# Second attention of an eight-sample transformer block: the product of probabilities and keys in groups of 3, 3, 3 and 4 row tiles

## The reference

```python
q_hk = (hidden_q @ Wq.T).reshape(b, s, H, K)
q_big = jnp.einsum('bshk,hkq->bshq', q_hk, w_kc_q)
kv_rope = kv_c * cos[None] + _rotate_half(kv_c) * sin[None]
q_r = jnp.einsum('bshq,hqr->bhsr', q_big, W_qr)
k_r = jnp.einsum('bld,hdr->bhlr', kv_rope, W_kr)
scores = jnp.einsum('bhsr,bhlr->bhsl', q_r, k_r)
attn = jax.nn.softmax(scores, axis=-1)
ctx_c = jnp.einsum('bhsl,bld->bhsd', attn, kv_rope)
ctx_lat = jnp.einsum('bhsd,hkd->bshk', ctx_c, w_kc_kv)
out = ctx_lat.reshape(b, s, H * K) @ Wo.T
```

## Time and profile before

| what | us |
|---|---|
| median of 3 runs (lowest to highest) | 866.58 (866.45 to 871.25) |
| profiled execution | 868.13 |
| its span, first to last instruction | 866.3 |
| TensorE busy in the span | 718.5 (83%) |
| VectorE, ScalarE, GpSimd busy | 510.5, 416.7, 248.4 |
| second attention, first score tile to first fold matmul | 427.78 to 664.15 |

### The profile page before, as it was taken

The page is one execution under the profiler, slowest core; times in us unless marked ns, Lnnn a source line. Parts: engine busy times, 40 slices in busy tenths (PEclk is TensorE's granted clock), DMA queues, the critical chain, the costliest instruction groups (busy, mean ns, idle before and its releaser), DMA issues.

```text
span 866.3 us, 13037 instructions
## 1 busy us (share of the span) xinstructions
PE 718.5 (83%) x4421; PEld 566.6 (65%) x4427; DVE 510.5 (59%) x1037; ACT 416.7 (48%) x777; POOL 248.4 (29%) x279
## 2 busy tenths in 40 slices
PE   0799999636999999985989989989996688799974
PEld 0597777425777777875868778778774265566541
DVE  4876675675666666156664564663663333677683
ACT  3523665345555555212575574664674312455552
POOL 2000931222112220342183282372451000122232
PEclk9987999667999999965999999999999789999997
DMA  8546732896675555983001212222425781111000
GB/s 260 200 173 202 256 106 85 294 343 234 206 228 176 167 163 164 332 220 105 2 25 45 63 44 63 63 55 51 130 66 109 246 358 67 50 50 37 13 25 15
DMA packets 82932, 118.90 MB, mean 137 GB/s; under 512 B 41761, under 2 KB 59933, under 8 KB 79297
## 3 DMA queue, kind: packets, MB, share of 16 engines
q1 hardware_dynamic: 79745, 109.71, 39.5%
q0 software_dynamic: 3136, 8.53, 3.7%
HBM read 97.15 MB, written 27.62 MB: 144 GB/s over the span
## 4 chain that ended last, share of the span: by engine, by line
PE 44%; issue 23%; DVE 11%; POOL 9%; ACT 6%; DMA 5%; SPq 1%; ACTq 1%; POOLq 0%; DVEq 0%
PE PS L149 9%; PE PS L151 8%; PE PS L150 8%; POOL wraw L818 6%; PE PS L1225 3%; PE PS L1286 3%; PE PS L1572 2%; DMA fq_raw<-foldq_in 2%; ACT w_hi L871 2%; PE PS L1329 2%; DMA raw<-wkv_in 1%; PE PS L1538 1%; ACT cx_hi L1113 1%; PE PS L1269 1%; PE PS L1318 1%
## 5 line engine op out<-in xcount | busy, mean ns | idle before, releaser
L818 POOL TENSOR_TENSOR wraw<-wraw,rinv 128x361 f32<-128x361 f32 (+1 forms) x104 | 80.8, 790 | 138.9 <-DVE rinv L1786 138.9
L1629 DVE TENSOR_TENSOR w_lo<-w,w_hi 128x1408 fp32r<-128x1408 f32 x40 | 65.0, 1625 | 38.5 <-ACT w_hi L871 38.5
L967 ACT ACTIVATE wraw<-PS,nmx 128x361 f32<-128x361 f32 (+1 forms) x104 | 58.7, 565 | 38.2 <-DVE nmx L1793 30.4
L1793 DVE TENSOR_REDUCE nmx<-PS 128x1 f32<-128x361 f32 (+1 forms) x104 | 55.0, 530 | 33.6 <-PE PS L151 33.6
L846 POOL TENSOR_TENSOR wraw<-gs,us 128x352 f32<-128x352 f32 (+1 forms) x28 | 26.6, 951 | 153.6 <-ACT gs L1141 125.9
L871 ACT CAST w_hi<-w 128x1408 fp32r x40 | 54.7, 1370 | 18.9 <-issue 9.8
L770 POOL DMA_INDIRECT xb<-xn_scratch,rows x20 | 32.7, 1634 | 105.4 <-PE PS L1197 102.3
L149 PE MATMUL PS<-w_hi,xt_hi 128*128 128x352 f32 x160 | 56.7, 355 | 6.2 <-DVE xt_lo L1623 6.0
L1796 DVE TENSOR_TENSOR pt_lo<-PS,pt_hi 128x384 fp32r<-128x384 f32 x96 | 52.3, 547 | 12.0 <-ACT pt_hi L973 11.1
L149 PE MATMUL PS<-pf_hi,cx_hi 128*128 128x512 f32 (+1 forms) x112 | 48.3, 431 | 11.5 <-DVE pf_lo L1964 4.5
L1385 PE MATMUL PS<-ident,wraw 128*128 128x128 f32 x312 | 52.1, 277 | 6.4 <-POOL wraw L818 3.7
(11 more groups left out here) (277 smaller groups left out, 1996.0 us busy)
## 6 DMA issues: line engine op xcount, KB each, us to landing
w<-w_in SPq DMA_DIRECT2D x20, 768.0 KB, 5.6
w<-w_in SPq DMA_DIRECT2D x8, 1408.0 KB, 11.3
fq_raw<-foldq_in SPq DMA_DIRECT2D x6, 1088.0 KB, 7.6
ctx_scratch<-ctxo SPq DMA_DIRECT2D x24, 256.0 KB, 2.1
cx_raw<-tile_scratch SPq DMA_DIRECT2D x6, 1024.0 KB, 4.9
ys_scratch<-yb SPq DMA_DIRECT2D x20, 256.0 KB, 5.6
wraw<-wup_in SPq DMA_DIRECT2D x12, 256.0 KB, 4.3
w1q<-w_scratch SPq DMA_DIRECT2D x1, 2816.0 KB, 11.2
```

The costliest lines, as they stand in the source:

```text
L818: pool.tensor_tensor(P1[slot][0:rows, 0:NK], P1[slot][0:rows, 0:NK], rinv[0:rows, jj, t:t + 1].broadcast_to((rows, NK)), ALU.mult).then_in ...
L967: act.activation(P1[t % 8][r, 0:NK], PS[r, t % 4, 0:NK], ACT.Exp, bias=nmx[r, jj, t:t + 1], accum_out=rsum[r, jj, t:t + 1]).then_inc(C["ex ...
L1629: dve.tensor_tensor(WL[which][:, :], w12_of(dve_wlo.e, which), WH[which][:, :].bitcast(F32), ALU.subtract) \
L1793: dve.tensor_reduce(nmx[r, jj, t:t + 1], PS[r, t % 4, 0:NK], AX.X, ALU.max, negate=True).then_inc(C["max"], 1)
```

## The change

The groups hold 3, 3, 3 and 4 tiles: 384, 384, 384 and 448 columns. `group_of` and `group_cols` give the group of a tile and its width. The third pair of buffers is dropped, and the two others are 448 columns wide and alternate by group number (g % 2); since NG stays 4, each batch begins with buffer 0. ScalarE waits for buffer g % 2 until the product of group g - 2 is done. Thirds of the first three groups stand two, three and four steps behind the turn of tiles 2, 5 and 8; those of the last group 4 steps behind tile 12, all in one step, as before. The stores have 384 or 448 columns.

```diff
-NG = -(-RT // 4)
+NG = RT // 3
...
-        PTH = [sc_(f"pt_hi{i}", [128, LK, 512], F32R) for i in range(2)]
-        PTL = [sc_(f"pt_lo{i}", [128, LK, 512], F32R) for i in range(2)]
-        PTH.append(sc_("pt_hi_end", [128, LK, ROWS % 512], F32R))
-        PTL.append(sc_("pt_lo_end", [128, LK, ROWS % 512], F32R))
+        PTH = [sc_(f"pt_hi{i}", [128, LK, ROWS - 384 * (NG - 1)], F32R) for i in range(2)]
+        PTL = [sc_(f"pt_lo{i}", [128, LK, ROWS - 384 * (NG - 1)], F32R) for i in range(2)]
...
-                    if t % 4 == 3:
-                        due += [(at + PVLAG + c, 0, ("PV", b, t // 4 * LK + c)) for c in range(LK)]
-                    elif t == RT - 1:
-                        due += [(at + PVLAG + 2, 0, ("PV", b, t // 4 * LK + c)) for c in range(LK)]
+                    if t == RT - 1:
+                        due += [(at + PVLAG + 2, 0, ("PV", b, (NG - 1) * LK + c)) for c in range(LK)]
+                    elif t % 3 == 2 and t // 3 < NG - 1:
+                        due += [(at + PVLAG + c, 0, ("PV", b, t // 3 * LK + c)) for c in range(LK)]
...
+        def group_of(t):
+
+            return min(t // 3, NG - 1)
+
+        def group_cols(g):
+
+            return ROWS - 384 * g if g == NG - 1 else 384
...
-                cols = min(512, ROWS - g * 512)
+                cols = group_cols(g)
...
-                    if t % 4 == 0:
-                        wait(act, C["pv"], pt_free(m, t // 4))
-                    act.copy(pt_place(PTH, t, jj), turned(t)).then_inc(C["pth"], 1)
+                    if t == 3 * group_of(t):
+                        wait(act, C["pv"], NG * m + group_of(t) - 1)
+                    act.copy(pt_place(PTH, t), turned(t)).then_inc(C["pth"], 1)
...
-                        wait(pe, C["ptl"], RT * m + min(4 * g + 4, RT))
+                        wait(pe, C["ptl"], RT * m + (3 * g + 3 if g < NG - 1 else RT))
                         wait(pe, C["ctxo"], NG * m + g)
                         wait(pe, C["knl"], m + 1)
```

More of the change, by code:

```diff
@@ L649, in store_ctx @@
             def store_ctx(n, g):
-                cols = min(512, ROWS - g * 512)
+                cols = group_cols(g)
                 wait(sp, C["ctxo"], NG * n + g + 1)
                 dst = ctx_scratch[n] if isinstance(n, int) else ctx_scratch[bass.ds(n, 1)].rearrange("o p r -> (o p) r")
-                sp.dma_start(dst[:, g * 512:g * 512 + cols], ctxo[g % 2][:, 0:cols]).then_inc(C[f"st{g % 2}"], 16)
+                sp.dma_start(dst[:, g * 384:g * 384 + cols], ctxo[g % 2][:, 0:cols]).then_inc(C[f"st{g % 2}"], 16)
             def store_batch(n, j, more=True):
@@ L940, in turned, with pt_place @@
             return PS[:, 4 + t % 3, 0:LK * 128].rearrange("p (c r) -> p c r", c=LK)[:, :, 0:tile_rows(t)]
[L942 to L951, removed]
+        def pt_place(buf, t):
+            at = (t - 3 * group_of(t)) * 128
+            return buf[group_of(t) % 2][:, :, at:at + tile_rows(t)]
         def act_keys(act, n, j):
@@ L977, in act_steps @@
                         continue
-                    cols = min(512, ROWS - t * 512)
+                    cols = group_cols(t)
                     wait(act, C["pv"], NG * m + t + 1)
@@ L1395, in pe_steps @@
                     last = mm3(pe, PS[:, 7, 0:cols], KNH[jj][:, c, :], KNL[jj][:, c, :],
-                               PTH[pt_buffer(g, jj)][:, c, 0:cols], PTL[pt_buffer(g, jj)][:, c, 0:cols], c == 0, c == LK - 1)
+                               PTH[g % 2][:, c, 0:cols], PTL[g % 2][:, c, 0:cols], c == 0, c == LK - 1)
                     if c == LK - 1:
@@ L1795, in dve_steps @@
                     wait(dve, C["pth"], RT * m + t + 1)
-                    dve.tensor_tensor(pt_place(PTL, t, jj), turned(t), pt_place(PTH, t, jj).bitcast(F32), ALU.subtract) \
+                    dve.tensor_tensor(pt_place(PTL, t), turned(t), pt_place(PTH, t).bitcast(F32), ALU.subtract) \
                         .then_inc(C["ptl"], 1)
```

## The result

The kernel with the change takes 853.27 us (median of 6 runs, 850.48 to 855.62), the one before 867.26 in the same comparison (866.45 to 871.25). The ratio is 0.9835, with a 95% interval of 0.9807 to 0.9863: 1.65% faster, where 1.5% was forecast (853.2 against 866.58). In a second comparison, later, it was 851.08 against 867.11, ratio 0.9825 (0.9787 to 0.9864).

What follows compares the result with a forecast made beforehand. TensorE was taken as the first resource, with 5 us of waits per pair. Pairs -3 x 1.2 - 1.4, query steps -3 x 2.1 and tail -2.1 sum to -13.4: 853.2 us against 866.58, forecast range 850 to 857.5, chance 0.6.

Steps and rivals of the forecast that it cites:

- The columns: TensorE's product matmuls: 384 columns take 0.176 us and 448 take 0.202, saving 0.66 us per batch, 5.3 in eight.
- The query steps: Preparation of the next pair's queries, three times: fewer thirds among 64-row matmuls; -2.1 us each, bounds -0.9 and -3.4.
- step 30: Within a pair's query work, numbered 26 to 37: one more product third stands here, +0.5 us.
- The score steps: Score tiles of a pair, numbered 0 to 25: -1.2 us per pair, bounds -0.3 and -2.0; -1.4 in the last pair.
- step 18: Turn 0 of the second batch, at about 516.0 as before; from here through 21, 5.40 us becomes 4.3, sum -1.0.
- steps 22 to 25: End of a pair's score tiles: one third more, a low-half wait gone, four shorter thirds; sum -0.2 us.
- Step 12: Second batch's first score tile waits for the exponential of the last tile, 2.14 us regardless of TensorE's work; sum 0.
- steps 13 to 18: Around the change of batch: low-half waits of 0.46 and 1.04 us go, bank 7 waits replace them; sum 0.
- The tail: Last score tile to fold, once: 12.7 us becomes about 10.5, sum -2.1, bounds -1.2 and -3.0.
- Only the columns: Rival for the whole stage: waits are conserved and only 5.3 us of work is saved; 861.3 us, chance 0.15.
- The partial gain: Rival: query work and tail gain as reckoned, four score stages nothing because ScalarE sets the pace; 858.2 us, chance 0.16.
- The slower rival: Bank 7 waits at group starts: at 1.1 us each the gain is gone, at 1.5 it is 875.2; chance 0.05.

Runs made afterwards that it cites:

- query_late: The changed kernel with the second batch's third-group thirds put back late among the 64-row query matmuls in the first three pairs; 856.28 us, ratio 0.9891.
- turns_on: The changed kernel with the three banks of turned tiles taken in turn across the change of batch, the keys' bank with them; 848.20 us, ratio 0.9794.
- tail_late: The changed kernel with the last pair's second-batch third-group thirds late, the first ahead of turn 12 and the others behind it; 849.13 us, ratio 0.9806.
- two_thirds: The changed kernel with the thirds of a group of three at offsets 0, 1, 1 instead of 0, 1, 2; 855.56 us, ratio 0.9873.

## Why the prediction was right, point by point

- **The columns.** Right, row by row: 0.176 and 0.203 us against the forecast of 0.176 and 0.202. The 64-column matmuls cost nearly half of a 512-column one, and merging them away was worth what the rows said. The Trainium skill, "TensorE: Matmul & The Clock Gate", section "Back-to-back issue gap", would give 0.1625 and 0.189 by its formula for single matmuls, lower than what this trace has for both widths. The prediction set that formula against a stream of matmuls, for which the page does not mean it: for a stream of weight load and matmul it gives about 0.131 at 512 columns. That too is lower than the 0.230 here.
- **The query steps.** Mechanism right, size too small: -2.66 each instead of -2.1. Up to the first 64-row step it was +0.03, as said (13.64 before, 13.67 after). Behind it the measured value is -2.70. The term that was mis-sized is the third among 64-row steps: "I take 1.1 each, -3.3". It came to 1.74 - 0.58 = 1.16 each, and the wait of 0.36 went with it, 3.84 in all. query_late confirms this for 384 columns, 0.99 each. The upper price of 1.42 was a misreading: the two rows that "start 0.32 apart" (482.81, 483.13) are not the starts of two query steps one after the other, but of two that overlap; undisturbed, a step takes 0.58 on average, not 0.32. The group's new third at step 30 cost 0.64 instead of 0.5, and the end +0.67, as taken. These make -2.53. Of the 0.17 that is left, 0.10 is in the same place: from 482.81 to 489.91 before and from 484.98 to 488.13 after, the stretch shrank by 3.95 and not 3.84, since the last three query steps now stand in a row and take 0.50 each (486.62 to 488.13), not 0.58.
- **The score steps.** Right in sign and mostly in the places, too large: -0.97, -0.99 and, in the last pair, -0.84, for -1.2, -1.2 and -1.4. The parts behind step 18 hit: 5.40 became 4.35 (515.14 to 519.49) where 4.3 was forecast, and steps 22 to 25 gave -0.23 for -0.2. Step 12 came out even, as said: the first score tile of the second batch starts 15.28 after S0 before and 15.30 after. What failed is the walk through steps 13 to 18, which ends in "So turn 0 of the second batch comes at about 516.0, as before": it came 0.31 later, counted from S0 (25.08 for 24.77). I had put bank 7 in the place of the vanished waits. Its waits came (0.33, 0.61, 0.33, for "0.5, and 0.8 at step 15"), but what holds turn 0 is the bank of turned tiles that it shares with turn 12, one step ahead. I had looked for what is late next on the product's path only; the turn itself had a second condition, met 0.24 us earlier in the kernel before and so without a wait in any view. VectorE's timeline of the kernel before has it:

```profile
515.36 0.34 DVE L1796 TENSOR_TENSOR pt_lo_end<-PS,pt_hi_end 128x192 fp32r<-128x192 f32 x1
```

  It ends at 515.70, and turn 0 starts at 515.94. The same subtraction in the changed kernel:

```profile
514.63 0.36 DVE L1795 TENSOR_TENSOR pt_lo<-PS,pt_hi 128x192 fp32r<-128x192 f32 x1 [0.23 <-ACT pt_hi L972]
```

  It ends at 514.99, and turn 0 starts at 515.14. Counted from S0, turn 12 itself stands 0.75 us later than before (22.71 for 21.96), behind three thirds more and the waits of 0.33 and 0.61 for bank 7. turns_on, which gives turn 0 another bank, removes the wait.
- **The first pair** gave -0.06 instead of -1.2, and that is the clock: in 425 to 435 us TensorE was granted 0.69 after and 0.83 before. In the repeated run of the changed kernel, where it was 0.83 too, the first pair took 37.34, 1.1 less than before; in query_late, where it was 1.00 throughout the first pair, it took 36.66. The windows of the changed kernel, then of its repeated run:

```profile
425.00:435.00 10.00, 8.59 (x49) 8.02 (x48) 7.29 (x19) 6.89 (x17) 2.71 (x4) 0.69 0.01 2
```

```profile
425.00:435.00 10.00, 8.75 (x44) 8.09 (x45) 7.78 (x24) 8.11 (x24) 7.27 (x10) 0.83 0.01 2
```

- **The tail.** Right, -2.09 for -2.1, and for the reason given. The last group began at 8.66 us after the last score tile where 8.6 was estimated. What I did not see is that the early place is not the best one (tail_late).
- **Outside the stage** +1.6 and -1.7 us cancel; both are in code that the change does not touch. In the repeated run the first S0 came at 425.43, 2.35 earlier than that of the kernel before, so the +1.6 is scatter.
- **The sum** of -13.4 met -13.0 because the score steps fell short by 2.1 us (of which 1.1 in the first pair) and the query steps ran over by 1.7. That the total was hit within 0.1 us is luck, since the two medians of the changed kernel (853.27, 851.08) lie 2.2 apart; the signs and the places are not.
- **The rivals.** "Only the columns" had the score steps nearly right (PE's busy time fell by 0.7 per pair, the idle time by 0.3) but falls with the query steps. The partial gain (no gain in the four score stages, because ScalarE sets the pace) falls with the 0.8 to 1.0 us that three of the four gained, and its reason falls with turns_on, where another 1.54 came from a bank alone. The slower rival asked for waits of 1.1 at each start of a group on bank 7; the longest was 0.61, and two_thirds, which has none of these waits, gains nothing.
- **A sign that was badly chosen.** The prediction asked for "the second pair's first score tile at 487.9 instead of 491.17" and took "behind 489.5" as the sign that the columns were nearly all. It came at 490.06 and by this sign the forecast was wrong. In the repeated run it came at 485.07. An absolute time carries all the scatter ahead of it. The distance between the S0 of two pairs is free of it in the later ones: 62.84 before, 59.20 after, -3.6 for a forecast of -3.3.

## What to carry to other kernels

When a wait disappears, list every condition of the instructions behind it, also those met just in time: one that is met 0.2 us before it is needed shows in no view, and takes over as soon as the first one goes. Rings of buffers that start again at 0 with each batch are such conditions wherever the batch's length is not a multiple of the ring; letting them run on cost no instruction here and gave 2.2 us per pair. The ring that gave most of it, that of the turned tiles, gave nothing at all before the regrouping; the other two were not tried there. And in a chain of single-file turns, independent work belongs behind the last of them, where it covers the copy, not between them.

## What the runs showed of the hardware

- A 128-row product between 64-row matmuls costs nearly twice its own time: 0.99 us for 0.53 (384 columns, query_late), 1.16 for 0.69 (512, before).
- Two neighbouring query steps, on different halves of the rows, run partly side by side: matmuls 0.01 us apart (485.29, 485.30 in the changed kernel) and 1.16 us for both, against 0.84 for one that stands alone (query_late). A product between them ends that, which is part of its price.
- The granted clock at the start of the stage differs from run to run of the same kernel (0.69 and 0.83 in 425 to 435 us for the changed one; 1.00 in query_late). The first S0 lies between 424.2 and 429.4 us over all kernels. Inside the stage, at full clock, the same stretch repeats within 0.06 us. A difference of 0.4 us can be read there that the scatter of the total, 1.3 to 9.5 us, hides.
